# V products and output products taken once per two slots in an attention and expert kernel

## The reference

```
x = x + attention(layernorm(x), ctx, seg)      # 16 heads, latent keys and values of 64
x = x + mean of the 2 best of 8 experts(layernorm(x))

kv_c = ctx @ W_kvc;  v = kv_c @ W_uv                       # per head 128 wide
scores = (q_nope . k_nope + q_rope . k_rope) * scale, masked to 9 keys before seg
out = softmax(scores) @ v;  attention = concat(out) @ W_o
```

## Time and profile before

| | |
|---|---|
| time, median of 3 runs | 395.16 us (394.85 to 395.56) |
| span of the profiled execution | 391.2 us |
| its own time | not given apart from the span; the median is 4.0 us above the span |
| instructions | 10358 |
| PE busy | 354.0 us, 90% |
| PE weight loads busy | 289.2 us, 74% |
| DVE busy | 288.3 us, 74% |
| ACT busy | 264.0 us, 67% |
| POOL busy | 234.1 us, 60% |

### The profile page before, as it was taken

One profiled execution on the slowest core, in us unless ns is written; L12 is line 12 of the kernel. 1 busy time (PEld: TensorE's weight loads), 2 busy tenths in 40 slices (PEclk: granted clock), 3 DMA queues, 4 the chain that ended last, 5 costly groups with the idle time before them and its releaser, 6 DMA issues.

```text
span 391.2 us, 10358 instructions
## 1 busy us (share of the span) xinstructions
PE 354.0 (90%) x2507; PEld 289.2 (74%) x2507; DVE 288.3 (74%) x1395; ACT 264.0 (67%) x907; POOL 234.1 (60%) x326
## 2 busy tenths in 40 slices
PE   1989999998999999999999999999998788999940
PEld 0856877786688878888878888788886577888730
DVE  2367887788888889888788888888889566444455
ACT  1347777788878878778888788788787544445430
POOL 4616555468976777677677676776764355455500
PEclk9999999999999999999999999999999999999985
DMA  8964040000000000000000000000000354543178
GB/s 277 349 215 188 7 105 3 1 3 29 0 30 1 30 20 7 27 0 27 14 14 27 0 27 0 27 27 0 30 2 28 95 161 131 148 132 121 34 239 316
DMA packets 15093, 28.27 MB, mean 72 GB/s; under 512 B 2892, under 2 KB 10719, under 8 KB 14416
## 3 DMA queue, kind: packets, MB, share of 16 engines
q1 hardware_dynamic: 11408, 20.25, 16.1%
q0 software_dynamic: 2960, 6.94, 5.0%
q10 hardware_dynamic: 688, 0.64, 0.6%
HBM read 17.81 MB, written 10.91 MB: 73 GB/s over the span
## 4 chain that ended last, share of the span: by engine, by line
PE 65%; DVE 12%; issue 10%; POOL 7%; DMA 2%; ACT 2%; DVEq 0%; SPq 0%; POOLq 0%; ACTq 0%
PE psum L1133 11%; PE psum L672 8%; PE psum L673 8%; PE psum L674 8%; PE psum L1090 7%; PE psum L1203 6%; PE psum L1117 5%; POOL prob L1361 2%; DVE x_all L1554 2%; POOL q_sb L1347 2%; PE psum L1180 2%; DVE nsc L1622 2%; DMA wcat<-in_w_kvc 2%; PE psum L369 2%; PE psum L1012 1%
## 5 line engine op out<-in xcount | busy, mean ns | idle before, releaser
L1228 ACT ACTIVATE prob<-nsc,nmax 128x128 f32<-128x128 f32 x256 | 100.8, 396 | 36.3 <-DVE nmax L1622 35.5
L1347 POOL TENSOR_TENSOR q_sb<-rope_a,rope_b 128x256 f32<-128x256 f32 x64 | 47.5, 742 | 59.2 <-DVE rope_b L1585 55.1
L1361 POOL TENSOR_TENSOR prob<-prob,prec 128x512 f32<-128x512 f32 x64 | 67.2, 1050 | 7.4 <-DVE prec L1593 7.4
L1133 PE MATMUL psum<-kT_all,qT 128*128 (+1 forms) x512 | 68.6, 277 | 1.1 <-ACT qT L1271 1.1
L1622 DVE CUSTOM_DVE_ANT_0 nsc<-psum,mask 128x128 f32<-128x128 f32 x256 | 58.6, 284 | 13.0 <-PE psum L1133 13.0
L1133 PEld LDWEIGHTS psum<-kT_all,qT 128*128 128x128 f32 x512 | 62.1, 192 | 2.7 <-ACT qT L1271 2.4
L1415 POOL DMA_INDIRECT halves<-jout,jidx x33 | 32.2, 976 | 30.3 <-DVE jidx L1526 13.7
L1228 ACT ACTIVATION_READ_ACCUMULATOR prob<-nsc,nmax 128x1 f32 x256 | 48.4, 189 | 0.0
L1090 PE MATMUL psum<-ident,q_sb 128*128 128x128 f32 x256 | 41.9, 286 | 2.2 <-POOL q_sb L1347 1.8
L1090 PEld LDWEIGHTS psum<-ident,q_sb 128*128 128x128 f32 x256 | 26.8, 140 | 21.7 <-POOL q_sb L1347 13.6
L1203 PE MATMUL psum<-pT,v_cur 128*64 128x256 f32 x256 | 41.8, 405 | 0.0
(11 more groups left out here) (204 smaller groups left out, 878.1 us busy)
## 6 DMA issues: line engine op xcount, KB each, us to landing
wanted<-slots SPq DMA_DIRECT2D x33, 129.0 KB, 2.4
wo_raw<-in_w_o SPq DMA_DIRECT2D x2, 1024.0 KB, 14.9
we_raw<-in_expert_w SPq DMA_DIRECT2D x1, 2048.0 KB, 7.8
half<-halves SPq DMA_DIRECT2D x4, 512.0 KB, 7.1
x_all<-in_x SPq DMA_DIRECT2D x2, 640.0 KB, 17.4
slots<-pad_row SPq DMA_DIRECT2D x8, 129.0 KB, 3.4
we_raw<-in_ctx_near SPq DMA_DIRECT2D x1, 1024.0 KB, 11.2
out<-x_all SPq DMA_DIRECT2D x2, 512.0 KB, 4.6
```

Of the source, the lines that this page charges most:

```text
L1133: mm = pe.matmul(B_S[r][:, h, :], qT[r][:, h, :], batch_keys, start=True, stop=True)
L1228: e = act.activation(prob[r][:, h, :], nsc[r][:, h, :], ACT.Exp, bias=nmax[r][:, h:h + 1], scale=-1.0, accum_out=psum_h[r][:, h:h + 1])
L1347: pool.tensor_tensor(q_sb[1 - r][:, :, KVC:P], rope_a[1 - r][:], rope_b[1 - r][:], ALU.add).then_inc(m["rope_joined"], 1)
L1361: pool.tensor_tensor(p[:], p[:], prec[1 - r][:, :].unsqueeze(2).to_broadcast([P, HG, P]), ALU.mult).then_inc(m["prob_normed"], 1)
```

## The change

V is done only in odd slots, for the two groups i - 3 and i - 2 at once: each of the two matmuls has 512 moving columns and fills the whole bank. ACT then copies 512 columns of B_O in the odd slot, and DVE makes 512 columns of oT_lo in the even slot after it. Y is done only in even slots, for groups i - 4 and i - 3: 12 matmuls (or 4 in the plain form). pT, oT_hi, oT_lo and oT are one buffer each for a pair, in place of two for one group each. PLAIN becomes 12. The semaphores pv_done, oT_done, oT_lo_done and y_done count pairs. Cut to its core:

```
-        PLAIN = 13
+        PLAIN = 12
+        def pair_of(b, k):
+            return (SLOTS // 2) * b + k // 2
...
 PE:
-                if live(i - 3, GROUPS):
-                    at_least(pe, "oT_done", i - 2)
+                if k % 2 == 0 and live(i - 4, GROUPS):
+                    gp, p = (k - 4) % GPT, pair_of(b, k - 4)
+                    at_least(pe, "oT_done", p + 1)
+                    if not plain(i - 4):
+                        pe.wait_ge(m["oT_lo_done"], p + 1 - PLAIN // 2)
...
-                    for q in range(2):
+                    for q in range(4):
...
-                if live(i - 2, GROUPS):
+                if k % 2 == 1 and live(i - 3, GROUPS):
+                    p = pair_of(b, k - 3)
...
                     at_least(pe, "pT_sb", i - 1)
-                    at_least(pe, "oT_done", i - 2)
+                    at_least(pe, "oT_done", p)
                     for odd in range(2):
-                        mm = pe.matmul(B_O[KVC * odd:KVC * odd + KVC, 0:D], v_cur[:], pT[r][:, odd::2, :],
-                                       start=True, stop=True)
+                        mm = pe.matmul(B_O[KVC * odd:KVC * odd + KVC, :], v_cur[:], pT[:, odd::2, :], start=True, stop=True)
 ACT:
-                    at_least(act, "pv_done", i - 3)
-                    act.copy(pT[r][:], B_PT[:, :].rearrange("p (h n) -> p h n", h=HG)).then_inc(m["pT_sb"], 1)
+                    at_least(act, "pv_done", pair_of(b, k - 2))
+                    act.copy(pT[:, HG * r:HG * r + HG, :], B_PT[:, :].rearrange("p (h n) -> p h n", h=HG)).then_inc(m["pT_sb"], 1)
...
-                if live(i - 2, GROUPS):
-                    at_least(act, "pv_done", i - 1)
-                    at_least(act, "y_done", i - 3)
-                    cols = oT[r][:] if plain(i - 2) else oT_hi[r][:]
-                    act.copy(cols, B_O[:, 0:D].rearrange("p (q n) -> p q n", q=2)).then_inc(m["oT_done"], 1)
+                if k % 2 == 1 and live(i - 3, GROUPS):
+                    p = pair_of(b, k - 3)
+                    at_least(act, "pv_done", p + 1)
+                    at_least(act, "y_done", p)
+                    cols = oT[:] if plain(i - 3) else oT_hi[:]
+                    act.copy(cols, B_O.rearrange("p (q n) -> p q n", q=4)).then_inc(m["oT_done"], 1)
 DVE:
-                if live(i - 3, GROUPS) and not plain(i - 3):
-                    at_least(dve, "oT_done", i - 2)
-                    at_least(dve, "y_done", i - 4)
-                    dve.tensor_tensor(oT_lo[1 - r][:], B_O[:, 0:D].rearrange("p (q n) -> p q n", q=2),
-                                      oT_hi[1 - r][:].bitcast(F32), ALU.subtract).then_inc(m["oT_lo_done"], 1)
+                if k % 2 == 0 and live(i - 4, GROUPS) and not plain(i - 4):
+                    p = pair_of(b, k - 4)
+                    at_least(dve, "oT_done", p + 1)
+                    at_least(dve, "y_done", p)
+                    dve.tensor_tensor(oT_lo[:], B_O.rearrange("p (q n) -> p q n", q=4), oT_hi[:].bitcast(F32),
+                                      ALU.subtract).then_inc(m["oT_lo_done"], 1)
```

More of the change, by code:

```diff
@@ L216, in kernel_program @@
         prec = [sb(f"prec{i}", [P, HG]) for i in range(2)]
-        pT = [sb(f"pT{i}", [P, HG, P]) for i in range(2)]
-        oT_hi = [sb(f"oT_hi{i}", [P, 2, P], F32R) for i in range(2)]
+        pT = sb("pT", [P, 2 * HG, P])
+        oT_hi = sb("oT_hi", [P, 4, P], F32R)
         plain_mem = ExitStack()
-        oT = [plain_mem.enter_context(nc.sbuf_tensor(f"oT{i}", [P, 2, P], F32)) for i in range(2)]
+        oT = plain_mem.enter_context(nc.sbuf_tensor("oT", [P, 4, P], F32))
         plain_mem.close()
-        oT_lo = [sb(f"oT_lo{i}", [P, 2, P], F32R) for i in range(2)]
+        oT_lo = sb("oT_lo", [P, 4, P], F32R)
         m_after, m_before = sb("m_after", [P, P]), sb("m_before", [P, P])
@@ L1049, in dense @@
                 if f == 0:
-                    pe.wait_ge(m["oT_lo_done"], GROUPS - PLAIN)
+                    pe.wait_ge(m["oT_lo_done"], (GROUPS - PLAIN) // 2)
                 elif f == 1:
@@ L1164, in slot @@
                     fold_o(pe, 3)
-                if live(i - 3, GROUPS):
-                    gp = (k - 3) % GPT
-                    at_least(pe, "oT_done", i - 2)
-                    if not plain(i - 3):
-                        pe.wait_ge(m["oT_lo_done"], i - 2 - PLAIN)
-                    if isinstance(i, int) and i - 3 < FOLDS:
+                if k % 2 == 0 and live(i - 4, GROUPS):
[3 more added lines that the diff above has]
+                        pe.wait_ge(m["oT_lo_done"], p + 1 - PLAIN // 2)
+                    if isinstance(i, int) and i - 4 < FOLDS:
                         pe.wait_ge(m["wo_done"], FOLDS)
@@ L1175, in slot @@
                     if gp == 0:
-                        at_least(pe, "x2_done", TPB * b + (k - 3) // GPT)
-                    for q in range(2):
[L1178 to L1181, removed]
+                        at_least(pe, "x2_done", TPB * b + (k - 4) // GPT)
+                    for q in range(4):
+                        first, last = gp == 0 and q == 0, gp == GPT - 2 and q == 3
+                        if plain(i - 4):
+                            mm = pe.matmul(B_Y[:, 0:D], oT[:, q, :], wo_all[:, 2 * gp + q, :], start=first, stop=last)
                         else:
-                            mm = mm3(pe, B_Y[:, 0:D], oT_hi[1 - r][:, q, :], oT_lo[1 - r][:, q, :], wo_hi[:, 2 * gp + q, :],
+                            mm = mm3(pe, B_Y[:, 0:D], oT_hi[:, q, :], oT_lo[:, q, :], wo_hi[:, 2 * gp + q, :],
                                      wo_lo[:, 2 * gp + q, :], start=first, stop=last)
@@ L1191, in slot @@
                     x_turn(pe, i)
-                if live(i - 2, GROUPS):
-                    if (k - 2) % SLOTS == 0:
-                        at_least(pe, "v_ready", b + (k - 2) // SLOTS + 1)
+                if k % 2 == 1 and live(i - 3, GROUPS):
+                    p = pair_of(b, k - 3)
+                    if (k - 3) % SLOTS == 0:
+                        at_least(pe, "v_ready", b + (k - 3) // SLOTS + 1)
                     at_least(pe, "pT_sb", i - 1)
-                    at_least(pe, "oT_done", i - 2)
-                    if not plain(i - 3):
-                        pe.wait_ge(m["oT_lo_done"], i - 2 - PLAIN)
-                    if isinstance(i, int) and i == 2:
+                    at_least(pe, "oT_done", p)
+                    if not plain(i - 4):
+                        pe.wait_ge(m["oT_lo_done"], p - PLAIN // 2)
+                    if isinstance(i, int) and i == 3:
                         pe.wait_ge(m["wo_done"], 2)
                     for odd in range(2):
-                        mm = pe.matmul(B_O[KVC * odd:KVC * odd + KVC, 0:D], v_cur[:], pT[r][:, odd::2, :],
-                                       start=True, stop=True)
+                        mm = pe.matmul(B_O[KVC * odd:KVC * odd + KVC, :], v_cur[:], pT[:, odd::2, :], start=True, stop=True)
                     mm.then_inc(m["pv_done"], 1)
@@ L1594, in slot @@
                 if (k - 2) % SLOTS == 0 and live(bv, B):
-                    at_least(dve, "pv_done", SLOTS * bv)
+                    at_least(dve, "pv_done", (SLOTS // 2) * bv)
                     if isinstance(bv, int) and bv == 0:
@@ L1628, in slot @@
                 if g == 2 and live(t - 1, TILES):
-                    at_least(dve, "y_done", GPT * t)
+                    at_least(dve, "y_done", (GPT // 2) * t)
                     dve.tensor_tensor(x2_of(t - 1), B_Y[:, 0:D], x2_of(t - 1), ALU.add).then_inc(m["x2_done"], 1)
```

## The result

The kernel after takes 406.6 us (403.52 to 407.97, 5 runs) against 395.56 us for the kernel before on the same chip. The ratio is 1.0268, with a 95% interval of 1.0234 to 1.0302: 10.6 us slower. 400.0 us was predicted, with a range of 395.0 to 402.5. The direction was right, the size was not. The profiled spans differ by the same amount: 401.8 against 391.2 us.

What follows compares the result with a forecast made beforehand. A serial DVE and POOL chain, level with PE's own work, was taken as the bound. Opening -0.4, 11 tiles +4.7 and tail +0.5 gave +4.8: span 391.2 to 396.0, plus 4.0 makes 400.0 us, range 395.0 to 402.5.

Steps and rivals of the forecast that it cites:

- 0.43: Forecast growth of one steady tile in us, from oT_lo's longer time on two DVE and POOL chains; bounds 0 and 0.7.
- V product and oT_lo: Forecast operation times: a pair's V product on PE 1.01 us; DVE's 512-column oT_lo 0.692 us, 0.27 more than at 256.
- PE's saving: The joined V product takes 0.25 us less PE time per pair, worth nothing while POOL delivers q_sb when it does.
- S(19) to QT(22), 10.83 + 0.27: From slot 19's score products to slot 22's query transposes: a serial DVE and POOL chain of 10.83 us, growing 0.27.
- QT(22) to QT(23), 3.93 + 0.27 against PE's 4.05, +0.16: Between query transposes of slots 22 and 23: second chain grows to 4.20, beating PE's 4.05, adding 0.16 us per tile.
- PE's slack of 0.11: Before the change, QT(22) to QT(23) takes 4.04 us on PE and at least 3.93 on the second chain.
- More than both: Rival: DVE's addition to x waits for 12 output matmuls and the wide ACT copy delays scores; 404 us, chance 0.12.
- Wide ACT copy, "into a slack of about 0.3": In steady tiles, ACT's 512-column copy ahead of the qT copy moves qT by some 0.2 us, within slack.
- Opening, -0.4: Slots before S(11): fewer V products, most of the gain given back in slots 6 to 11; -0.4 us, between -1.7 and 0.
- Tail, +0.5: Last slots: later oT_lo in slot 62 and later output products in slot 66; +0.5 us, between 0 and +1.6.
- The 4.0 us above the span: Median run time 395.16 us lies 4.0 above the profiled span, taken as launch and end, untouched by the change.
- My upper bound for a tile, 0.7: Upper bound in us for a steady tile's growth, beside the forecast 0.43 and the lower bound 0.

Runs made afterwards that it cites:

- e5: The kernel before, with DVE's oT_lo in even slots working its 256 columns twice (one 512-column operation, result unused): 401.87 us, ratio 1.0147.
- e13: e10 with ACT's 512-column copy of the V result moved to the next slot, behind the qT copy: 386.99 us, ratio 0.9757 against the kernel before.
- e9: The kernel after, with the second of POOL's two scatters moved from slot g = 0 to g = 1: 392.6 us, ratio 0.9888 against the kernel before.
- e10: The kernel after, with oT_lo behind rope products and reciprocal, its matmuls last, and POOL's second scatter moved to slot g = 1: 393.07 us.
- e1: The kernel before with only the output products joined, 12 matmuls per even slot; V product, ACT copy and oT_lo per slot: 412.26 us, ratio 1.0402.

## Why the prediction was right or wrong

The direction and the place were right; the size was not. By the profiled spans +4.8 was forecast and +10.6 measured. Of the missing 5.8, 2.5 are in the steady tiles (0.65 per tile against 0.43), 1.2 in the opening, 1.1 in the tail and 1.0 ahead of S(1).

- **V product and oT_lo:** right, 1.01 and 0.687 us. PE's saving is worth nothing in the steady tiles of the kernel after: right.
- **S(19) to QT(22), 10.83 + 0.27:** the mechanism was right and the term was mis-sized: 11.30. The failed step is "S(19) to QT(22) is one serial chain", which hangs the chain on S(19). row starts when POOL's rstd ends (124.58 and 124.72), and rstd follows POOL's join and prob for slot 20. They follow DVE's rope_b of slot 19, which DVE reaches in its own order behind the oT_lo of slot 18, whatever PE's S(19) does. So the stretches that I added up are parts of one ring over DVE and POOL: in e5 DVE comes from the oT_lo of slot 22 to row in slot 23 with no wait for PE on this path.
- **QT(22) to QT(23), 3.93 + 0.27 against PE's 4.05, +0.16:** the distance was right (4.23 in e5), the sum was not. I took off PE's slack of 0.11 in each tile. PE's slack is used up once; the DVE and POOL ring grows by 2 x 0.27 = 0.54 in each tile. The 0.11 comes back as a row that starts 0.10 later after S(g = 3) in e5. 0.43 became 0.59, of which 0.05 stays open: 1.6 of the missing 5.8 us, over ten tiles.
- **"More than both" had a chance of 0.12:** part of it is there. DVE's addition to x waits 0.34 for the 12 output matmuls (not at all in e5), and the kernel after has 17.28 per tile where e5, with oT_lo's growth alone, has 17.17: about 1.1 us over ten tiles (the first of the eleven grew by 0.18 only). That this wait is the cause is read from the trace and was not tested by itself.
- **Wide ACT copy, "into a slack of about 0.3":** the slack was not there. QT(20) to S(20) went from 1.64 to 1.79, by a mean of 0.20 over the steady slots g = 0. It was hidden in the tile all the same, since the join for g = 2 set the tile whatever qT did. It was no longer so once the chains were short: the copy's move gave 6 us in e13.
- **Opening, -0.4:** wrong sign, +0.8 from S(1) on. 0.6 of it is the wait for q_sb at QT(14), a scatter slot that I had left out of the chain's price; e9 and e10 take it away. Another 1.0 ahead of S(1) is the granted clock of the profiled run, not the change.
- **Tail, +0.5:** +1.6; e5 has +1.3 with no wide V or ACT work, so it is mostly the later oT_lo of the last slots. From S(63) to the end the profiled runs range from 88.4 to some 94 us. All above 90 have a mean granted clock of 0.94 to 0.97 between S(63) and 40 us ahead of the end; the kernels before and after and e5 have 1.00 there (88.56, 89.62 and 89.27), so these three can be compared.
- **The 4.0 us above the span** is not all launch and end. In every run with both numbers on record the time is 1.7 to 1.9 above the span of the same execution; so the profiled execution of the kernel before must have been some 2 us faster than the median. It changes nothing in the difference forecast.
- **The bounds.** My upper bound for a tile, 0.7, held the measured 0.65 (0.70 over the last ten). The range ended at 402.5 because I gave the sizes above 0.43 too little; three terms erred on one side together.

## What to carry to other kernels

When chains close into a ring over engines that need not wait for PE, add the growth at every place of the ring per turn, and subtract PE's slack once, not in every turn. Before work is joined into wider operations, ask for each engine what stands right behind the wide one: the place of one instruction was worth 14 us for a scatter on POOL and 6 us for a copy ahead of qT on ACT, against some 8 us for the joined V product by the prediction's own sum. Parts of a change that balance each other can't be priced one by one: e1 cost 16 us and the whole 11.

## What the runs showed of the hardware

gt, a 128x8 DVE operation with a scalar from SBUF, took 1.57 us in the kernel after, where POOL's join and prob follow each other without a gap: it started at 131.89, ahead of prob (132.37), and was held over both. In e13 it comes when prob (161.37 for 1.04) is as good as over, and takes 0.22, with a scatter following at 162.56. Its row in the timeline of DVE:

```profile
162.34 0.22 DVE L1460 TENSOR_SCALAR gt<-logit,top 128x8 f32<-128x8 f32 x1
```

So the size of a small DVE operation gives no hint of its price: over the 16 tiles its mean went from 1.21 us to 0.42 when one scatter was moved (e9), with nothing changed on DVE.
